# Delta rule in a two-layer fp32 kernel: decay products of levels 0 to 4 as packed 32 by 32 strips, put into the matrices by transfers; merges at 16 and 32 as 64 by 64 diagonal tiles

## The chip, the core and the metric

One core of a Trainium2 chip runs the whole program. It has TensorE (PE, with its weight loads shown apart as PEld), VectorE (DVE), ScalarE (ACT), GpSimd (POOL) and SyncE (SP), which issues every transfer here. The metric is the device time of one launch in microseconds (us): 1788.34 us as the median of three runs (1781.23, 1788.34, 1789.08).

## The reference, cut to what matters

The program is two layers on x of 1024 tokens by 256: windowed attention and a feed-forward block, then delta-rule attention and feed-forward, all in fp32. The change lies in the delta rule of layer 1, with 16 heads of width 128, whose recurrence is per token

```
S   = S * exp(g_t)[:, None]          # decay of each key channel
u_t = beta_t * (v_t - k_t^T S)       # the delta
S   = S + k_t u_t^T
o_t = q_t^T S
```

The kernel takes 128 tokens at a time (a chunk, 8 per head). In a chunk it needs two triangular matrices per head and chunk: M, of products of key i with key j and the decay between them, and the same with query i. Then it needs the inverse of (1 + M), since each delta depends on those before it.

## The kernel before, in words

**The decay products by levels.** A decay between two tokens is a product over the channels and can't be taken as one factor outside the matmul. So the matrix is built in 7 levels: at level lv the tokens are grouped into pairs of runs of s = 2^lv tokens, and only the block (left run, right run) of each pair is computed. After each level, `advance` multiplies the keys and queries by the decay of a run, so that the next level's product is right. Before, levels 0 to 5 were computed as 64 by 64 diagonal pieces of a 128-token chunk: `dr_level` on PE (L849) makes, for a group `gr` of four chunks, 8 matmuls with 64 columns of stationary keys each, two per chunk (they go to the upper and the lower 64 partitions of the bank). Each moves 64 columns (32 for keys and 32 for queries). PE runs an fp32 matmul as two passes, so the trace shows 16 instructions for it. DVE then picks, with a predicated copy under a mask (L1597), the blocks of the level out of 512 columns of the bank into MB, the matrix tile, for levels 0 to 4. Levels 5 and 6 are copied by ACT. `advance` is L1617 and L1619 on DVE. The two groups alternate, group 0 in bank 2 and group 1 in bank 3.

**The base inverse.** After level 3 the 16 by 16 diagonal blocks are complete. SP writes the 64 of them (8 chunks by 8 blocks) to DRAM in 8 transfers (L519) and reads them back (L523) as 64 rows, one block per partition. DVE inverts all 64 together in 29 short steps (`invert` L1697, `less` L1705 and L1708), ACT makes a transposed copy (`flip`, L1215). SP then writes both to DRAM (L531, L532) and puts them in 16 transfers (L538, L539) on the diagonals of XX (the inverse) and YY (its transpose).

**The merges.** From 16 the inverse grows to 32, 64 and 128: `left` (L869 at 16 and 32, L871 at 64) multiplies MB by XX, ACT negates the product into PM (L1201), `right` (L891 and L893, L887 at 64) multiplies that by YY and by XX's transpose, and DVE (L1636, L1639) copies the new blocks into XX and YY. At 16 and 32 these are matmuls over the full 128 by 128 array, 4 per `left` and 8 per `right` and group.

**The scan.** For each chunk in turn: `predict` (L912, L913), DVE subtracts (L1646), `solve` (L924), ACT copies (L1224), `update` (L931, L932), DVE adds (L1657).

**The order.** The order on each engine is written out by hand as the table `PLACE`: (time in heads, step), sorted over all heads, so steps of up to four heads stand beside each other. The engines wait for each other by semaphores, PE and DVE strictly in this order. SP has its own order, in `delta_rule_loads`: per head m, `zero` (waits for the last `left` of head m-1), `beta_of`, `head`, `blocks`, `inverse`, `gate_weights`. `inverse` waits for the last `less` and for `flip`. PE's `left` at 16 waits for the transfers of XX.

## Time and profile before

The profiled execution has a span of 1786.4 us, 1.9 us under the median of the three runs and between the lowest and the highest of them; what lies around its span isn't recorded apart.

| engine | busy us | share of the span |
|---|---|---|
| PE matmul | 1552.1 | 87% |
| PE weight load | 1073.6 | 60% |
| DVE | 1338.7 | 75% |
| ACT | 1034.0 | 58% |
| POOL | 41.3 | 2% |
| DMA queue of SP | - | 12.1% of 16 engines |

The delta rule takes from about 560 to 1710 us, and in its steady part a pair of heads takes 128.8 us. The program alternates between heads of even and of odd number, since the output projection is done every second head. A high busy share is an average: each stretch of a head has its own limit, so the rows below go by stretches. The clock that PE was granted is in the columns of the windows (1.00 is 2.4 GHz, 0.50 is 1.2 GHz).

### The profile page before, as it was taken

What the parts mean: (1) busy time and instruction counts of PE and PEld (TensorE: products, weight loads), DVE (VectorE), ACT (ScalarE), POOL (GpSimd) and SP (SyncE); (2) the same over time, 40 slices, a digit from 0 to 9 for tenths busy, and PEclk for the clock granted to TensorE, in tenths of its full rate; (3) what the DMA queues carried; (4) which work ended last, traced back from release to release, by engine and by line L of the source; (5) the groups of instructions that cost most, each with busy time, mean ns of one, the idle gap of its engine ahead of it and who ended that gap; (6) DMA issues with size and microseconds to landing.
All of it is one profiled execution on the core that took longest, in us unless ns stands there. A gap on an engine that the chain in (4) does not pass through costs nothing. (4 is left out here: it accounts for less than half of the span.)

```text
span 1786.4 us, 33061 instructions
## 1 busy us (share of the span) xinstructions
PE 1552.1 (87%) x10840; PEld 1073.6 (60%) x10840; DVE 1338.7 (75%) x3718; ACT 1034.0 (58%) x2716; POOL 41.3 (2%) x49
## 2 busy tenths in 40 slices
PE   6887888788797689999999999999899999988678
PEld 3434555564453256776776776677677677677435
DVE  5859989847722578989888898898998988983131
ACT  5428778766311556776586676676667657643210
POOL 0000000000000000000000000000000000000000
PEclk9989999899998789999999999999999999978589
DMA  3041000000101101101111110110110110100010
GB/s 152 25 100 49 8 10 4 2 1 1 74 0 40 66 12 41 55 11 57 59 23 45 58 56 11 57 56 12 61 54 16 57 54 15 45 28 7 0 50 24
DMA packets 83350, 66.79 MB, mean 37 GB/s; under 512 B 58592, under 2 KB 72160, under 8 KB 82032
## 3 DMA queue, kind: packets, MB, share of 16 engines
q1 hardware_dynamic: 83184, 64.69, 12.1%
q8 instruction: 91, 1.49, 0.4%
q14 instruction: 75, 0.61, 0.1%
HBM read 55.71 MB, written 6.98 MB: 35 GB/s over the span
## 5 line engine op out<-in xcount | busy, mean ns | idle before, releaser
L796 PE MATMUL bank<-xt,arena 128*128 128x512 f32 x384 | 204.7, 669 | 4.5 <-ACT arena L1106 3.1
L1539 DVE SCALAR_TENSOR_TENSOR arena<-arena 128x1024 f32<-128x1024 f32 x144 | 184.1, 1279 | 31.7 <-ACT arena L1114 30.9
L1597 DVE COPY_PREDICATED arena<-arena,bank 128x512 f32<-128x512 int32 x160 | 185.1, 1176 | 0.0
L849 PE MATMUL bank<-arena 128*64 128x64 f32 x3072 | 143.6, 238 | 36.8 <-DVE arena L1619 22.3
L849 PEld LDWEIGHTS bank<-arena 128*64 128x64 f32 x3072 | 116.9, 144 | 84.3 <-issue 55.4
L1617 DVE TENSOR_TENSOR arena<-arena 128x512 f32<-128x512 f32 x224 | 156.6, 699 | 3.8 <-PE bank L849 3.0
L646 PE MATMUL bank<-xt,arena 128*128 128x512 f32 x320 | 142.6, 602 | 3.8 <-DVE arena L1357 3.8
L796 PEld LDWEIGHTS bank<-xt,arena 128*128 128x128 f32 x384 | 76.2, 215 | 79.2 <-issue 76.4
L1113 ACT COPY arena<-bank 128x512 f32<-128x512 f32 x96 | 56.6, 589 | 99.0 <-PE bank L796 99.0
L646 PEld LDWEIGHTS bank<-xt,arena 128*128 128x128 f32 x320 | 60.4, 193 | 86.8 <-issue 86.6
L1047 ACT ACTIVATE arena<-arena 128x128 f32<-128x128 f32 x256 | 99.1, 389 | 6.6 <-DVE arena L1467 6.6
L665 PE MATMUL bank<-arena 128*128 128x256 f32 (+2 forms) x384 | 95.6, 395 | 6.2 <-DVE arena L1357 5.3
L893 PE MATMUL bank<-arena 128*128 128x64 f32 x512 | 99.5, 275 | 0.0
L891 PE MATMUL bank<-arena 128*128 128x64 f32 x512 | 96.5, 269 | 0.8 <-DVE arena L1639 0.5
L1224 ACT COPY arena<-bank 128x128 f32<-128x128 f32 x128 | 34.3, 268 | 104.6 <-PE bank L924 104.2
L1619 DVE TENSOR_TENSOR arena<-arena 128x256 f32<-128x256 f32 x224 | 94.3, 421 | 0.0
L1233 ACT COPY arena<-bank 128x128 f32<-128x128 f32 x128 | 34.1, 267 | 96.5 <-PE bank L932 59.2
L665 PEld LDWEIGHTS bank<-arena 128*128 128x128 f32 (+2 forms) x384 | 67.9, 189 | 34.8 <-issue 20.5
L693 PE MATMUL bank<-xt,arena 128*128 128x512 f32 x160 | 83.1, 648 | 5.3 <-DVE arena L1450 4.5
L891 PEld LDWEIGHTS bank<-arena 128*128 128x128 f32 x512 | 80.4, 194 | 9.7 <-DVE arena L1639 5.9
L912 PEld LDWEIGHTS bank<-arena 128*128 128x128 f32 x224 | 40.8, 199 | 67.1 <-issue 39.4
L893 PEld LDWEIGHTS bank<-arena 128*128 128x128 f32 x512 | 78.8, 194 | 0.0
(169 smaller groups left out, 3512.3 us busy)
## 6 DMA issues: line engine op xcount, KB each, us to landing
arena<-zero_scratch SPq DMA_DIRECT2D x29, 512.0 KB, 4.3
arena<-d_w SPq DMA_DIRECT2D x16, 519.0 KB, 6.2
arena<-beta_scratch SPq DMA_DIRECT2D x16, 512.0 KB, 5.5
arena<-w_scratch SPq DMA_DIRECT2D x2, 1376.0 KB, 6.1
arena<-f_idx SPq DMA_DIRECT2D x2, 1072.0 KB, 12.5
w_scratch<-arena SPq DMA_DIRECT2D x2, 1072.0 KB, 4.0
arena<-a_wq SPq DMA_DIRECT2D x16, 128.0 KB, 2.8
arena<-a_wo SPq DMA_DIRECT2D x1, 2048.0 KB, 10.8
```

Source lines behind the costliest of these rows:

```text
L646: last = pe.matmul(bank[2 * w + n % 2][0:rows, :], (WU if f < 2 else WU1R)[:, w, k, m * P:m * P + rows], XT[:, k, hf * HALF:(hf + 1) * HAL ...
L665: last = pe.matmul(bank[4 + pair][:, j * D:(j + 1) * D], HT[0:rows, hf, m, t * P:(t + 1) * P], (WD if f < 2 else WD1)[0:rows, m, :], start ...
L693: last = pe.matmul(bank[6 + m % 2][:], w, XT[:, k, hf * HALF:(hf + 1) * HALF], start=(k == 0), stop=(k == KC - 1))
L796: last = pe.matmul(bank[b][:], DW[:, par, c:c + P], XT[:, k, rhs], start=(k == 0), stop=(k == KC - 1))
L849: last = pe.matmul(to[:, :, p], KL[:, par, r], rhs, start=True, stop=True)
L891: pe.matmul(to[:, 0], YY[:, par, c, :], PM[:, c, :].rearrange("p (b r s) -> p b r s", r=2, s=s)[:, :, 0, :], start=True, stop=True)
L893: last = pe.matmul(to[:, 1], PM[:, c, :], YY[:, par, c, :].rearrange("p (b r s) -> p b r s", r=2, s=s)[:, :, 1, :], start=True, stop=True)
L1047: last = act.activation(EX[:, p % 2, i, a, :], SMK[:, p % 2, i, a, :], ACT.Exp, bias=NMX[:, p % 2, i, a:a + 1], scale=-1.0, accum_out=ES[: ...
L1539: dve.scalar_tensor_tensor(out=CT[:, x], in0=RAW[:, x, 3 - j:3 - j + S], scalar=DW[:, par, tap:tap + 1], in1=CT[:, x], op0=ALU.mult, op1=A ...
L1597: dve.copy_predicated(out, mask, bank[b][:].rearrange("p (c b s) -> p c b s", c=8, s=s)).then_inc(free[b], 1)
L1617: dve.tensor_tensor(kq, kq, left, ALU.mult)
L1619: dve.tensor_tensor(kl, kl, t[:, :, 1, :].broadcast_to([P, nb // 2, s]), ALU.mult).then_inc(kq_step, 1)
```

## The change

The matrices MB stay as they are, but levels 0 to 4 are computed into a packed tile MBC. A chunk of 128 tokens is four strips of 32 tokens, and strip k of the diagonal stands on partitions 32k to 32k+31, 32 columns wide. On PE a level is 16 matmuls per group instead of 8, each with 32 columns of stationary keys (to one quarter of the bank's partitions) and 32 moving columns. On DVE the predicated copy reads 128 columns instead of 512. After level 4, SP puts the strips into MB by four transfers of 32 partitions (`strips`), which stand between `blocks` and `inverse`. `left` at 16 waits for them too.

XX and PM keep only the two 64 by 64 diagonal blocks (64 columns). The merges at 16 and 32 are done per 64 by 64 block: `left` is 8 matmuls per group with 64 rows, 64 stationary and 64 moving columns instead of 4 over the full array, `right` is 16 with 64 rows, 64 stationary and 32 moving columns instead of 8. ACT's negation reads 256 columns instead of 512. DVE's copy into XX is 128 columns instead of 256, and the one into YY becomes two of 64 partitions by 128 columns. The masks are cut out of the input by eight small transfers instead of one. `PLACE` doesn't change.

```diff
@@ -42,6 +42,10 @@
 BASE = 4
 BLK = 1 << BASE
 NB = P // BLK
+STRIP = 2 * BLK
+HP = P // 2
+DR_CONST = 16 * (2 + P // STRIP + 4)
+STRIP_LEVELS = BASE + 1
 
...
         MB = A.take(2, NT, 2, P)
+        MBC = A.take(2, NT, 2, STRIP)
         YY = A.take(2, NT, P)
-        XX = A.take(NT, P)
-        PM = A.take(NT, P)
+        XX = A.take(NT, HP)
+        PM = A.take(NT, HP)
         VB = A.take(2, NT, P)
         KT = A.take(2, NT, P)
...
                     sp.dma_start(BL, blk_in.rearrange("b (j i) -> b j i", j=BLK)).then_inc(blocks_in, 16)
+
+                def strips(m, par):
+
+                    sp.wait_ge(strips_ready, 2 * m + 2)
+                    wait(sp, full[6], read(6, m - 2, "predict", NT - 1))
+                    for k in range(P // STRIP):
+                        ks = slice(STRIP * k, STRIP * (k + 1))
+                        sp.dma_start(MB[ks, par, :, :, ks], MBC[ks, par]).then_inc(strips_put, 16)
 
                 def inverse(m, par):
 
...
+                    strips(m, m % 2)
                     inverse(m, m % 2)
                     if m + 2 < H:
...
@@ -841,6 +864,13 @@
                     pe.wait_ge(kq_step, done("dve", n, "advance", lv - 1, gr))
                 for t in range(4):
                     c = 4 * gr + t
+                    if lv < STRIP_LEVELS:
+                        for k in range(P // STRIP):
+                            r = slice(c * P + STRIP * k, c * P + STRIP * (k + 1))
+                            rhs = KQ[:, par, :, r].rearrange("p w (b r s) -> p w b r s", r=2, s=s)[:, :, :, 1, :]
+                            to = bank[b][STRIP * k:STRIP * (k + 1), t * STRIP:(t + 1) * STRIP]
+                            last = pe.matmul(to.rearrange("p (w b s) -> p w b s", w=2, s=s), KL[:, par, r], rhs, start=True, stop=True)
+                        continue
                     if lv < LEVELS - 1:
                         for p in range(2):
                             r = slice(c * P + 64 * p, c * P + 64 * p + 64)
...
                     pe.wait_ge(x_put, 16 * NB * (n + 1))
-                    for high in range(BASE, LEVELS):
+                    pe.wait_ge(strips_put, 16 * (P // STRIP) * (n + 1))
+                    for high in range(STRIP_LEVELS, LEVELS):
                         pe.wait_ge(free[b], read(b, n, "level", high, gr))
                 else:
                     pe.wait_ge(x_sel, done("dve", n, "right", lv - 1, gr))
                 for t in range(4):
                     c = 4 * gr + t
                     if lv < LEVELS - 1:
-                        last = pe.matmul(bank[b][:, t * P:(t + 1) * P], MB[:, par, c, 0, :], XX[:, c, :], start=True, stop=True)
+                        for h in range(2):
+                            hs = slice(HP * h, HP * (h + 1))
+                            last = pe.matmul(bank[b][hs, t * HP:(t + 1) * HP], MB[hs, par, c, 0, hs], XX[hs, c, :],
+                                             start=True, stop=True)
                     else:
-                        last = pe.matmul(bank[b][64:P, t * 64:(t + 1) * 64], MB[0:64, par, c, 0, 64:P], XX[0:64, c, 0:64],
+                        last = pe.matmul(bank[b][HP:P, t * HP:(t + 1) * HP], MB[0:HP, par, c, 0, HP:P], XX[0:HP, c, :],
                                          start=True, stop=True)
                 last.then_inc(full[b], 1)
 
...
                     if lv == LEVELS - 1:
-                        last = pe.matmul(bank[4][0:64, t * 64:(t + 1) * 64], PM[64:P, c, 0:64], YY[64:P, par, c, 64:P],
+                        last = pe.matmul(bank[4][0:HP, t * HP:(t + 1) * HP], PM[HP:P, c, :], YY[HP:P, par, c, HP:P],
                                          start=True, stop=True)
                         continue
-                    to = bank[4][:, t * P:(t + 1) * P].rearrange("p (w b s) -> p w b s", w=2, s=s)
-                    pe.matmul(to[:, 0], YY[:, par, c, :], PM[:, c, :].rearrange("p (b r s) -> p b r s", r=2, s=s)[:, :, 0, :],
-                              start=True, stop=True)
-                    last = pe.matmul(to[:, 1], PM[:, c, :], YY[:, par, c, :].rearrange("p (b r s) -> p b r s", r=2, s=s)[:, :, 1, :],
-                                     start=True, stop=True)
+                    for w in range(2):
+                        for h in range(2):
+                            hs = slice(HP * h, HP * (h + 1))
+                            y = YY[hs, par, c, hs]
+                            to = bank[4][hs, t * HP + STRIP * w:t * HP + STRIP * (w + 1)].rearrange("p (b s) -> p b s", s=s)
+                            left, moved = (PM[hs, c, :], y) if w else (y, PM[hs, c, :])
+                            moved = moved.rearrange("p (b r s) -> p b r s", r=2, s=s)[:, :, w, :]
+                            last = pe.matmul(to, left, moved, start=True, stop=True)
                 last.then_inc(full[4], 1)
 
             def dr_keys(n, par, gr):
...
                 if lv < LEVELS - 1:
-                    act.mul(PM[:, cg, :], bank[b][:].rearrange("p (c k) -> p c k", c=4), -1.0).then_inc(free[b], 1)
+                    act.mul(PM[:, cg, :], bank[b][:, 0:4 * HP].rearrange("p (c k) -> p c k", c=4), -1.0).then_inc(free[b], 1)
                 else:
...
@@ -1582,22 +1619,22 @@
             def dr_level(n, par, lv, gr):
 
                 b = 2 + gr
-                dve.wait_ge(dr_const, 48)
+                dve.wait_ge(dr_const, DR_CONST)
                 dve.wait_ge(full[b], turn(b, n, "level", lv, gr) + 1)
                 if lv == 0:
-                    wait(dve, full[6], read(6, n - 2, "predict", NT - 1))
+                    wait(dve, strips_put, 16 * (P // STRIP) * (n - 1))
                 else:
                     dve.wait_ge(free[b], read(b, n, "level", lv - 1, gr))
                 if lv == BASE:
                     dve.wait_ge(blocks_out, 16 * NB * (n + 1))
                 s = 1 << lv
-                out = MB[:, par, 4 * gr:4 * gr + 4].rearrange("p c w (b r s) -> p (c w) b r s", r=2, s=s)[:, :, :, 1, :]
-                mask = MKU[:, lv, :].rearrange("p (a b s) -> p a b s", a=1, s=s).broadcast_to([P, 8, 64 // s, s])
+                out = MBC[:, par, 4 * gr:4 * gr + 4].rearrange("p c w (b r s) -> p (c w) b r s", r=2, s=s)[:, :, :, 1, :]
+                mask = MKC[:, lv, :].rearrange("p (a b s) -> p a b s", a=1, s=s).broadcast_to([P, 8, BLK // s, s])
                 dve.memset(TICK[:, 6 + 2 * lv + gr:7 + 2 * lv + gr], 0.0)
-                dve.copy_predicated(out, mask, bank[b][:].rearrange("p (c b s) -> p c b s", c=8, s=s)).then_inc(free[b], 1)
-                if lv == BASE - 1:
+                dve.copy_predicated(out, mask, bank[b][:, 0:4 * STRIP].rearrange("p (c b s) -> p c b s", c=8, s=s)).then_inc(free[b], 1)
...
+                if lv >= BASE - 1:
                     dve.wait_ge(free[b], read(b, n, "level", lv, gr))
-                    dve.memset(TICK[:, 18 + gr:19 + gr], 0.0).then_inc(blocks_ready, 1)
+                    dve.memset(TICK[:, 16 + 2 * (lv - BASE + 1) + gr:17 + 2 * (lv - BASE + 1) + gr], 0.0).then_inc((blocks_ready, strips_ready)[lv - BASE + 1], 1)
 
             def dr_advance(n, par, lv, gr):
...
@@ -1632,11 +1669,14 @@
                     dve.wait_ge(y_put, 16 * NB * (n + 1))
                 dve.memset(TICK[:, 18 + 2 * lv + gr:19 + 2 * lv + gr], 0.0)
                 x = XX[:, cg, :].rearrange("p c (b r s) -> p c b r s", r=2, s=s)[:, :, :, 0, :]
-                mask = MKL[:, lv, :].rearrange("p (a b s) -> p a b s", a=1, s=s).broadcast_to([P, 4, 64 // s, s])
+                mask = MKX[:, lv - BASE, :].rearrange("p (a b s) -> p a b s", a=1, s=s).broadcast_to([P, 4, STRIP // s, s])
                 dve.copy_predicated(x, mask, prod[:, :, 0]).then_inc(x_sel, 1)
-                y = YY[:, par, cg, :].rearrange("p c (b r s) -> p c b r s", r=2, s=s)[:, :, :, 1, :]
-                mask = MKU[:, lv, :].rearrange("p (a b s) -> p a b s", a=1, s=s).broadcast_to([P, 4, 64 // s, s])
-                dve.copy_predicated(y, mask, prod[:, :, 1]).then_inc(free[4], 1)
+                for h in range(2):
+                    hs = slice(HP * h, HP * (h + 1))
+                    y = YY[hs, par, cg, hs].rearrange("p c (b r s) -> p c b r s", r=2, s=s)[:, :, :, 1, :]
+                    mask = MKY[hs, lv - BASE, :].rearrange("p (a b s) -> p a b s", a=1, s=s).broadcast_to([HP, 4, STRIP // s, s])
+                    last = dve.copy_predicated(y, mask, prod[hs, :, 1])
+                last.then_inc(free[4], 1)
 
             def dr_predict(n, par, c):
```

SyncE around the transfers of one head (before; the third head of the delta rule). `blocks` is L519 and L523, `inverse` L531 to L539:

```order
68 L519 DMA block_scratch<-arena 16x8x16 [waits blocks_in,blocks_ready]
69 L519 DMA block_scratch<-arena 16x8x16 x7
70 L523 DMA arena<-block_scratch 64x256 [waits base_step,blocks_out]
71 L531 DMA inverse_scratch<-arena 64x256 [waits x_put,y_put,flipped,base_step]
72 L532 DMA inverse_turned_scratch<-arena 64x256
73 L538 DMA arena<-inverse_turned_scratch 16x8x16 [waits x_zero,inverse_out]
```

The same place now, with the strips as L545:

```order
71 L533 DMA block_scratch<-arena 16x8x16 [waits blocks_in,blocks_ready]
72 L533 DMA block_scratch<-arena 16x8x16 x7
73 L537 DMA arena<-block_scratch 64x256 [waits base_step,blocks_out]
74 L545 DMA arena<-arena 32x16x32 [waits strips_ready]
75 L545 DMA arena<-arena 32x16x32 x3
76 L553 DMA inverse_scratch<-arena 64x256 [waits x_put,y_put,flipped,base_step]
77 L554 DMA inverse_turned_scratch<-arena 64x256
78 L560 DMA arena<-inverse_turned_scratch 16x8x16 [waits x_zero,inverse_out]
```

The four transfers and their wait for level 4 now stand ahead of the inverse's way out to DRAM, and each has 32 by 16 pieces of 32 elements.

TensorE at the first merge of a head, before (bank2 and bank3 are `left` of the two groups, bank4 is `right`, bank5 and bank6 are the scan of another head):

```order
1104 L869 MATMUL bank2<-arena 128x128 x4
1105 L869 MATMUL bank3<-arena 128x128 x4
1106 L931 MATMUL bank5<-arena 128x128
1107 L932 MATMUL bank6<-arena 128x128
1108 L891 MATMUL bank4<-arena 128x64
1109 L893 MATMUL bank4<-arena 128x64
1110 L891 MATMUL bank4<-arena 128x64
1111 L893 MATMUL bank4<-arena 128x64
```

And now:

```order
964 L902 MATMUL bank2<-arena 64x64 x8
965 L902 MATMUL bank3<-arena 64x64 x8
966 L968 MATMUL bank5<-arena 128x128
967 L969 MATMUL bank6<-arena 128x128
968 L931 MATMUL bank4<-arena 64x32 x16
969 L835 MATMUL bank1<-arena 128x512
```

The steps stand in the same order; each `left` has twice the matmuls with half the columns, and so has each `right`, in runs of 16 (L931 now, L891 and L893 before).

## Rows read from the trace of the kernel before

**Rows 1.** Windows (us; then per engine busy us and count; then PEclk, DMA share, GB/s).

```profile
979.30:998.30 19.00, 19.00 (x148) 17.20 (x146) 14.67 (x30) 12.91 (x25) 0.00 (x0) 1.00 0.06 17
998.30:1015.70 17.40, 15.73 (x200) 12.05 (x199) 16.96 (x40) 10.34 (x26) 1.63 (x1) 1.00 0.34 123
1015.70:1044.40 28.70, 25.85 (x167) 16.42 (x166) 25.50 (x67) 19.96 (x47) 0.00 (x0) 0.94 0.11 15
1044.40:1059.90 15.50, 15.50 (x129) 14.15 (x128) 13.26 (x28) 12.58 (x25) 0.00 (x0) 1.00 0.02 5
1059.90:1077.40 17.50, 15.82 (x201) 12.10 (x199) 17.05 (x40) 10.34 (x26) 1.64 (x1) 1.00 0.34 122
1077.40:1108.10 30.70, 28.89 (x183) 19.41 (x182) 26.80 (x69) 20.43 (x47) 0.00 (x0) 0.94 0.10 15
```

**Rows 2.** Timeline of DVE: start us, us, line, operation, shapes, count.

```profile
983.57 0.51 DVE L1636 COPY_PREDICATED arena<-arena,bank 128x256 f32<-128x256 int32 x1
...
999.11 1.33 DVE L1597 COPY_PREDICATED arena<-arena,bank 128x512 f32<-128x512 int32 x1
1000.23 0.73 DVE L1617 TENSOR_TENSOR arena<-arena 128x512 f32<-128x512 f32 x1
...
1020.66 0.86 DVE L1597 COPY_PREDICATED arena<-arena,bank 128x512 f32<-128x512 int32 x1
```

**Rows 3.** Timeline of PE at 202 us (attention, tiles of 64 by 64).

```profile
201.48 0.67 PE L713 MATMUL bank<-arena 64*64 64x128 f32 x16
202.08 0.44 PE L726 MATMUL bank<-ident,arena 128*128 128x128 f32 x2
```

**Rows 4.** Timeline of PE, merges and levels.

```profile
986.65 1.06 PE L869 MATMUL bank<-arena 128*128 128x128 f32 x8
987.55 1.89 PE L958 MATMUL bank<-arena 128*128 128x256 f32 x8
...
992.34 0.33 PE L891 MATMUL bank<-arena 128*128 128x64 f32 x2
...
994.17 0.38 PE L938 MATMUL bank<-arena 128*1 128x128 f32 x2
...
1002.12 0.73 PE L849 MATMUL bank<-arena 128*64 128x64 f32 x16
1002.78 0.67 PE L887 MATMUL bank<-arena 64*64 64x64 f32 x8
1003.38 0.49 PE L924 MATMUL bank<-arena 128*128 128x128 f32 x2
...
1013.27 0.69 PE L849 MATMUL bank<-arena 128*64 128x64 f32 x16 [0.26 <-DVE arena L1619]
```

**Rows 5.** Timelines of SP, then DVE, then PE, around the inverse of one head.

```profile
1015.73 3.63 SPq L519 DMA_DIRECT2D block_scratch<-arena  x8
...
1033.07 0.45 SPq L531 DMA_DIRECT2D inverse_scratch<-arena  x1
...
1042.80 0.42 SPq L539 DMA_DIRECT2D arena<-inverse_scratch  x1
...
1031.46 0.18 DVE L1708 TENSOR_TENSOR arena<-arena 64x14 f32<-64x14 f32 x1
...
1034.11 0.86 DVE L1597 COPY_PREDICATED arena<-arena,bank 128x512 f32<-128x512 int32 x1
...
1044.38 1.80 PE L869 MATMUL bank<-arena 128*128 128x128 f32 x14
```

**Rows 6.** Line L587 on SP: transfers of 512 pieces (duration ns min/median/max, starts).

```profile
L587 SPq DMA_DIRECT2D arena<-arena x4: 652/1068/1200, 120.7 to 126.5; - x4
```

**Rows 7.** PE after its longest wait in the delta rule, and the clock there.

```profile
660.60 3.75 PE L869 MATMUL bank<-arena 128*128 128x128 f32 x16 [3.78 <-issue]
...
663.00:667.00 4.00, 4.00 (x21) 4.00 (x20) 0.00 (x0) 2.74 (x4) 0.00 (x0) 0.50 0.02 4
```

36 lines of the change are left out of this document (23 added, 13 removed).

## The prediction

> **What bounds the kernel now.** I read the windows of two neighbouring heads first, cut at three events: the first `left` at 16, the first level, and the way out of the 16 by 16 blocks [rows 1]. The pair takes 128.8 us. The reader is to see three stretches with three different limits. From `left` to level 0 (19.0 and 15.5 us) PE is busy without a gap. From level 0 to the blocks (17.4 and 17.5 us) DVE is busy for 16.96 of 17.40 and PE for 15.73. From the blocks to the next `left` (28.7 and 30.7 us) neither is full; there a chain runs: blocks out and in, 29 short DVE steps, inverse out, 16 transfers in, `left`. The timelines of SP, DVE and PE show that chain [rows 5]: blocks leave at 1015.73, the last `less` starts at 1031.46, the inverse leaves at 1033.07, the last transfer is issued at 1042.80, and `left` starts at 1044.38, which leaves 1.6 us for that transfer to land. So in this head PE arrives at `left` when the data does. The next head's stretch is 2 us longer, since it holds two more projections; PE comes last there.
>
> **The levels on DVE.** The predicated copy of 512 columns at level 0 keeps DVE from 999.11 to 1000.23, 1.12 us; at level 4, where runs are long, one lasts 0.86 us, and a copy of 256 columns of that kind 0.51 us [rows 2]. On that line 128 columns last 0.33 us; I take 0.3. Ten copies per head save 8 x 0.82 + 2 x 0.5 = 7.6 us of DVE, of which 6.6 lie in the stretch that DVE bounds. DVE is left with 10.4 us there, so PE is next.
>
> **The levels on PE.** A group of 16 passes costs 0.66 us, start to start (1002.12 to 1002.78) [rows 4]. It becomes 32 passes of half the columns, on four tiles. No row shows this form. The ends: if four tiles run at once and each pass costs by its columns, 32 passes take half of the 0.51 us that 16 take without the last one's own length, so 0.45 us with start and end. If a pass can't start more often than in the attention's group, 16 passes of 128 columns on four tiles in 0.67 us less 0.27 for the last [rows 3], 27 ns each, then 32 take 0.85 + 0.19 = 1.04 us. Below 0.45 it can't fall while the columns set it. I take the middle, 0.75 us, +0.09 per group. From level 0's start (998.3) to the last of the eight groups (1013.27) it is 15.0 us [rows 4], of which PE waits most of 1.7 [rows 1]. With DVE fast 1.2 of the wait goes: 15.0 - 1.2 + 7 x 0.09 = 14.4, and 1.1 us for that group and its copy (2.4 before, as DVE was behind). The stretch becomes 15.5 instead of 17.4.
>
> **The merges on PE.** `left` at 16 or 32 costs 0.90 us (986.65 to 987.55), `right` 1.83 us (992.34 to 994.17) [rows 4]. Now they run on two 64 by 64 tiles in turn. The nearest row is again the level group of two tiles with 64 columns: 0.66 us for 16 passes, so 0.66 for `left`, and 0.66 + 0.49 = 1.15 for the 32 passes of `right`, whose stationary part has 64 columns too. Four of each per head save 4 x 0.24 + 4 x 0.68 = 3.7 us. The other end, one tile after the other, is the rival below. In the stretch of 19.0 us this gives 15.3, and DVE's 14.67 lies close below, so 15.6; in the one of 15.5 PE would need 11.8, but DVE has 13.26, so 13.4. There DVE's extra copy into YY (two of 64 partitions instead of one, 0.3 each) and the smaller copy into XX cancel. ACT's negation gets shorter beside PE's work: nothing.
>
> **The new wait.** SP's queue goes: blocks, strips, inverse. The strips need level 4 of group 1, whose copy starts at 1034.11 [rows 5], 2.65 us after the last `less`; the inverse left at 1033.07. With a copy of 0.3 and its tick the strips can go at 1034.6, 1.5 us after the inverse left before. Then come four transfers of 512 pieces. The attention has such transfers (512 pieces, of 512 bytes): 0.65 us to issue the first, 1.07 in the middle, 1.20 at most [rows 6]. The last transfer of an inverse, with 128 pieces, took 0.42. The ends are 4 x 0.45 = 1.8 and 4 x 1.1 = 4.4; the pieces here are of 128 bytes and start on an idle queue, so I take 4 x 0.65 + gaps = 2.7. Behind the waiting instruction stand the inverse's two transfers, its 16, the weights of the gate and the zeroing for the next head; only the first two kinds are waited for, by `left`. Landing behind the strips' bytes I give 0.3 (0 to 2). DVE reaches the inversion earlier by the shorter copy at level 4 and what it waits less: 0.8 (0.5 to 1). Sum: 1.5 + 2.7 + 0.3 - 0.8 = +3.7, so 28.7 becomes 32.4 us, now in both heads. PE would come to `left` at 30.2 and 32.2 (28.7 and 30.7, plus 1.3 as the blocks leave sooner after PE's last group, plus 0.2 for two groups), so it is late by the chain by 2.2 and 0.2 us. What was PE's slack is gone.
>
> **The sum.** A pair: 15.6 + 13.4 + 2 x 15.5 + 2 x 32.4 = 124.8 us. To this 1 us for the clock: after a wait of 3.78 us PE ran at 0.50 for the whole of the next window, and two `left` took 3.75 us [rows 7] instead of twice 0.90. A wait of 2.2 us is shorter, so I charge little. 125.8 against 128.8 is 1.5 us per head, times 15 about 22 us. At the start eight small transfers for masks instead of one and a memset more cost about 1 us. The first and the last head have empty engines around; there the shorter levels and the longer chain cancel. The profiled execution has 1786.4 us of span, 1.9 below the median; I subtract from the latter: 1788 - 22 = **1766 us**.
>
> **Rival 1, the full gain.** The four tiles run at once (0.45 us per group) and the transfers cost 1.8 us. Then the second stretch is 13.4, the chain 31.4, and PE comes last at 32.2 in every second head: 29.0 + 26.8 + 63.6 = 119.4, 4.7 us per head, **1717 us**. For it: groups with two and with four tiles both go as their columns say. Against: nothing so far shows passes as short.
>
> **Rival 2, slower: the two diagonal tiles don't overlap.** The two tiles of a merge have different rows of the array and write the same bank. In the attention, tiles of different rows write different banks; the level groups have two tiles with the same rows. A group on one single tile (L887) takes 0.60 us for 8 passes, 1002.78 to 1003.38 [rows 4], 65 ns per pass. `left` then costs 1.12, `right` 2.16, and each stretch after `left` grows by 4 x 0.22 + 4 x 0.33 = 2.2 instead of shrinking: 21.2 + 17.7 + 31.0 + 64.8 = 134.7, 3 us per head, **1832 us**. It decides as soon as a merge pass goes above 50 ns, since then the 1.5 us of gain are spent. The Trainium skill has the rule behind it, "TensorEngine Tiling (Array Packing)", section "Restrictions and Gotchas": different row tiles can't access the same PSUM bank at the same time. By that rule the time is this rival's, without it the forecast's; no row here tests it, as the attention's code avoids the case.
>
> **Rival 3, slower: the wait takes over.** The transfers take 1.07 us each to issue and 2 us more to land: the chain is 35.9 us, PE waits over 3 us in each head, and the clock falls as in [rows 7]. 7 us more per pair and 2 for the clock: 133.8, 2.5 us per head, **1825 us**. For it: SP has nothing between the blocks and the inverse now, so each microsecond counts in full. Against: the pieces are a quarter of the attention's.
>
> **Rival 4, no gain: the passes don't get shorter.** At 1.04 us per level group the second stretch is 17.5 as before and PE comes to `left` later, which hides the chain: 129.4, **1793 us**. The even pace of 27 ns in [rows 3] speaks for it as much as for columns. The Trainium skill says the same from its side: "TensorE: Matmul & The Clock Gate", section "Wait — 56ns, not 53.3ns?", has a floor of about 25 ns from start to start however few the columns. By that floor 32 passes would be an estimated 0.99 us and the time this rival's; the trace shows 34 and 27 ns per pass, never less, so it doesn't refute it.
>
> **Chances.** Forecast 0.40 (its own range 1745 to 1785), rival 1 0.15, rival 2 0.15, rival 3 0.12, rival 4 0.18 (1775 to 1810). A difference under 0.5%, 9 us, is no change here. Faster: 0.32 + 0.15 + 0.05 = 0.52. Same: 0.08 + 0.02 + 0.07 = 0.17. Slower: 0.15 + 0.10 + 0.06 = 0.31. The range reaches from under rival 1 to rival 2, 1712 to 1832.
>
> **What would show it.** The predicated copy of the levels near 0.3 us; a level group's 32 passes in 0.45, 0.75 or 1.04 us; `left` in 0.66 and `right` in 1.15 us, or near 1.1 and 2.2; the first strip transfer 1.5 us after the inverse used to leave, 0.65 us each; PE idle right before `left` at 16, by 2 us in one head of two, and whether its clock falls after that. The stretch from blocks to `left` should be near 32 us in both heads. If it stays at 29 to 31, the wait was hidden; if DVE still fills the second stretch, its copies didn't shrink with the columns, and the forecast fails there.

## The result, and the profile after

The changed kernel takes 1813.8 us as the median (1797.3 to 1819.9), the kernel before 1788.7 (1781.2 to 1789.5): a ratio of 1.0134 with a 95% interval of 1.0083 to 1.0184. It is slower by 1.3%. The forecast was 1766 us, faster by 1.2%. The profiled execution has a span of 1813.3 us (1786.4 before).

The totals moved as they were meant to, and the time didn't follow. TensorE's matmuls are busy for 32 us less (1519.7), VectorE for 99 us less (1239.9). The page of the changed kernel, its line of the engines and one group (for the group: busy us and mean ns, then the idle time ahead of it and what ended that):

```profile
PE 1519.7 (84%) x14936; PEld 1014.4 (56%) x14936; DVE 1239.9 (68%) x3815; ACT 1025.5 (57%) x2716; POOL 41.2 (2%) x49
...
L902 PE MATMUL bank<-arena 64*64 64x64 f32 x1024 | 50.4, 258 | 58.0 <-issue 55.2
```

L902 is `left` at 16 and 32. TensorE stands idle for 58.0 us ahead of it, in the trace of before 4.9 us. That is a new wait of (58.0 - 4.9) / 15 = 3.5 us per head. The six windows of the same two heads show where it lies and what comes with it, against [rows 1] (columns as there: PE, PEld, DVE, ACT, POOL busy, then PEclk, DMA share, GB/s):

```profile
990.05:1006.87 16.82, 15.52 (x240) 12.37 (x241) 12.85 (x29) 12.82 (x26) 0.00 (x0) 1.00 0.08 22
1006.87:1020.32 13.45, 12.66 (x319) 9.46 (x319) 11.56 (x41) 9.29 (x25) 1.63 (x1) 1.00 0.40 141
1020.32:1053.39 33.07, 24.66 (x206) 16.08 (x205) 26.50 (x71) 20.42 (x48) 0.00 (x0) 0.97 0.14 21
1053.39:1069.87 16.48, 15.32 (x225) 12.12 (x225) 11.65 (x27) 11.45 (x24) 0.00 (x0) 0.76 0.02 5
1069.87:1087.24 17.37, 17.02 (x319) 12.70 (x319) 11.65 (x41) 10.68 (x26) 1.63 (x1) 0.71 0.32 109
1087.24:1122.16 34.92, 29.18 (x221) 19.84 (x221) 27.80 (x73) 20.80 (x48) 0.00 (x0) 0.95 0.13 20
```

The first two rows are what the change can do: 16.82 and 13.45 us, where before took 19.00 and 17.40, both at full clock. The third and sixth are the queue: 33.07 and 34.92 us for 28.70 and 30.70. The fourth and fifth are the same steps as the first two (the fourth has less to do, as in [rows 1]), at a granted clock of 0.76 and 0.71. They took 16.48 and 17.37, where before took 15.50 and 17.50, at 1.00.

Call the three stretches A (`left` at 16 to level 0), B (level 0 to the blocks) and C (blocks to `left`). To compare kernels I use their means over 13 heads (heads 2 to 14, counted from 0) of one trace each, with the time at the lower clock (PEclk 0.50, which is 1.2 GHz, against 1.00, which is 2.4 GHz) in brackets: 2 x (1 - PEclk) x the length of the window. The median is of all runs. The ratio to before is an estimate of its own, with an interval, and not the quotient of the two medians; it differs from that by up to 0.5%. One of the five runs of the strips from ACT (1765.1 us) counts as slow; without it their median is 1748 us.

| kernel | A | B | C | sum | median us | ratio |
|---|---|---|---|---|---|---|
| before | 17.1 (0) | 17.5 (0) | 29.7 (3.4) | 64.4 | 1789 | 1 |
| changed | 17.9 (7.1) | 15.1 (4.7) | 33.5 (2.2) | 66.5 | 1814 | 1.0134 |
| strips, old merges | 19.1 (4.0) | 13.3 (0) | 33.5 (2.0) | 65.8 | 1808 | 1.0093 |
| merges alone | 15.1 (0) | 19.8 (6.0) | 30.3 (3.6) | 65.1 | 1799 | 1.0055 |
| strips from ACT | 15.0 (0) | 16.0 (6.8) | 32.3 (2.9) | 63.3 | 1752 | 0.9741 |
| strips behind the inverse | 16.3 (3.4) | 16.0 (7.1) | 31.2 (1.1) | 63.4 | 1755 | 0.9769 |
| strips from POOL | 15.0 (0) | 15.8 (6.8) | 30.0 (0.5) | 60.8 | 1725 | 0.9617 |
| same, old merges | 17.1 (0) | 13.3 (0) | 29.5 (0.5) | 59.9 | 1718 | 0.9605 |
| strips from POOL, wait filled | 28.6 for both (0) | | 29.9 (0.8) | 58.5 | 1693 | 0.9471 |

### The profile page after: what moved, and what is told of

Same layout as the page of the kernel before. It is cut to its first block and busy times, and to the rows that moved or that the text cites. A ratio compares the mean times of both kernels' runs of the same rounds, so it can differ in the third digit from the quotient of the medians.

```text
span 1813.3 us, 41435 instructions
## 1 busy us (share of the span) xinstructions
PE 1519.7 (84%) x14936; PEld 1014.4 (56%) x14936; DVE 1239.9 (68%) x3815; ACT 1025.5 (57%) x2716; POOL 41.2 (2%) x49
## 5 line engine op out<-in xcount | busy, mean ns | idle before, releaser
L1576 DVE SCALAR_TENSOR_TENSOR arena<-arena 128x1024 f32<-128x1024 f32 x144 | 184.6, 1282 | 32.4 <-ACT arena L1151 31.0
L819 PE MATMUL bank<-xt,arena 128*128 128x512 f32 x384 | 195.3, 642 | 5.4 <-ACT arena L1143 4.0
L669 PE MATMUL bank<-xt,arena 128*128 128x512 f32 x320 | 143.3, 604 | 3.8 <-DVE arena L1394 3.8
L688 PE MATMUL bank<-arena 128*128 128x256 f32 (+2 forms) x384 | 100.2, 409 | 6.2 <-DVE arena L1394 5.3
L902 PE MATMUL bank<-arena 64*64 64x64 f32 x1024 | 50.4, 258 | 58.0 <-issue 55.2
L872 PEld LDWEIGHTS bank<-arena 128*32 128x32 f32 x5120 | 62.4, 120 | 65.4 <-issue 51.8
L1697 DVE SCALAR_TENSOR_TENSOR arena<-arena,bank 128x128 f32<-128x128 f32 x112 | 38.7, 345 | 87.0 <-PE bank L968 84.9
L872 PE MATMUL bank<-arena 128*32 128x32 f32 x5120 | 77.5, 209 | 23.2 <-DVE arena L1617 14.0
L949 PEld LDWEIGHTS bank<-arena 128*128 128x128 f32 x224 | 43.1, 213 | 89.8 <-issue 56.0
L931 PEld LDWEIGHTS bank<-arena 64*64 64x64 f32 x2048 | 79.3, 159 | 24.2 <-DVE arena L1678 14.6
L716 PE MATMUL bank<-xt,arena 128*128 128x512 f32 x160 | 87.5, 677 | 6.3 <-DVE arena L1487 5.6
L931 PE MATMUL bank<-arena 64*64 64x32 f32 x2048 | 86.1, 241 | 2.1 <-DVE arena L1678 2.0
L949 PE MATMUL bank<-arena 128*128 128x128 f32 x224 | 53.2, 323 | 38.1 <-DVE arena L1697 31.2
```

Source lines behind the costliest of these rows:

```text
L669: last = pe.matmul(bank[2 * w + n % 2][0:rows, :], (WU if f < 2 else WU1R)[:, w, k, m * P:m * P + rows], XT[:, k, hf * HALF:(hf + 1) * HAL ...
L688: last = pe.matmul(bank[4 + pair][:, j * D:(j + 1) * D], HT[0:rows, hf, m, t * P:(t + 1) * P], (WD if f < 2 else WD1)[0:rows, m, :], start ...
L716: last = pe.matmul(bank[6 + m % 2][:], w, XT[:, k, hf * HALF:(hf + 1) * HALF], start=(k == 0), stop=(k == KC - 1))
L819: last = pe.matmul(bank[b][:], DW[:, par, c:c + P], XT[:, k, rhs], start=(k == 0), stop=(k == KC - 1))
L872: last = pe.matmul(to.rearrange("p (w b s) -> p w b s", w=2, s=s), KL[:, par, r], rhs, start=True, stop=True)
L931: last = pe.matmul(to, left, moved, start=True, stop=True)
```

## The experiments

**Where the queue's time goes.** The timeline of SP of the changed kernel around the inverse of that head, against [rows 5]:

```profile
1020.32 3.63 SPq L533 DMA_DIRECT2D block_scratch<-arena  x8
...
1038.70 2.67 SPq L545 DMA_DIRECT2D arena<-arena  x4
1041.54 0.52 SPq L553 DMA_DIRECT2D inverse_scratch<-arena  x1
...
1044.17 0.31 SPq L560 DMA_DIRECT2D arena<-inverse_turned_scratch  x1
...
1052.13 0.43 SPq L561 DMA_DIRECT2D arena<-inverse_scratch  x1
```

The inverse leaves 21.2 us after the blocks (1041.54 - 1020.32) instead of 17.3 (1033.07 - 1015.73). TensorE then arrives early and waits, and what happens to its clock is in the timeline of PE and in four windows around it: the work before the wait, the wait, the work behind it, and work later in the same stretch.

```profile
1053.39 1.97 PE L902 MATMUL bank<-arena 64*64 64x64 f32 x32 [4.79 <-issue]
...
1063.97 0.68 PE L902 MATMUL bank<-arena 64*64 64x64 f32 x16
1064.49 1.07 PE L931 MATMUL bank<-arena 64*64 64x32 f32 x32
...
1069.87 0.49 PE L872 MATMUL bank<-arena 128*32 128x32 f32 x32 [1.16 <-DVE arena L1617]
```

```profile
1043.50:1048.60 5.10, 4.52 (x22) 2.94 (x22) 4.80 (x8) 4.00 (x9) 0.00 (x0) 1.00 0.15 20
1048.60:1053.39 4.79, 0.00 (x1) 0.04 (x1) 1.50 (x3) 0.27 (x1) 0.00 (x0) 0.77 0.19 18
1053.39:1061.14 7.75, 7.75 (x74) 6.09 (x74) 3.75 (x10) 3.75 (x8) 0.00 (x0) 0.50 0.04 9
1062.30:1068.50 6.20, 6.20 (x122) 4.82 (x118) 5.44 (x15) 5.29 (x13) 0.00 (x0) 1.00 0.00 0
```

The clock is 1.00 up to the wait, falls in it, and is 0.50 for 7.75 us of full work behind it. The price of the wait is therefore the 4.79 us of standing still and then up to half of those 7.75. The first six experiments take this apart.

**1. The wait alone, in the kernel before.** SP waits for level 4 and issues four transfers of unused data, and nothing gets shorter.

```diff
+                def strips(m, par):
+                    sp.wait_ge(strips_ready, 2 * m + 2)
+                    wait(sp, strips_put, 64 * m)
+                    for k in range(4):
+                        ks = slice(32 * k, 32 * (k + 1))
+                        sp.dma_start(JUNK[ks, :, :, ks], MBC[ks, par]).then_inc(strips_put, 16)
...
+                    strips(m, m % 2)
                     inverse(m, m % 2)
```

> The kernel before with nothing changed but SyncE's queue: between blocks and inverse it waits for level 4 of both groups and then issues four transfers of 512 pieces of 128 bytes each to a tile that nobody reads. Theory 1: blocks to left from 29.7 to about 34 us, TensorE stalls of 3 to 6 us before left, half clock after them, left to level 0 longer than 17.1 though nothing in it changed, by 1 to 4 us; time 1788 + 16 x 5 to 8 = 1870 to 1915 us. Theory 2 (the clock or a stall does no harm of its own): left to level 0 stays at 17.1, time at most 1788 + 16 x 4.5 = 1860.

Measured: 1886.5 us, ratio 1.0550 (1.0522 to 1.0577), +98 us. C grew from 29.7 to 34.1, and A from 17.1 to 19.3, with 4.4 us at the lower clock, though nothing in A was changed. The windows of one head (A, B, C):

```profile
1157.17:1177.81 20.64, 20.64 (x144) 18.84 (x144) 12.93 (x27) 12.65 (x24) 0.00 (x0) 0.92 0.07 17
1177.81:1195.29 17.48, 15.81 (x200) 12.12 (x198) 17.00 (x40) 10.35 (x26) 1.63 (x1) 0.99 0.34 122
1195.29:1230.01 34.72, 27.38 (x167) 17.76 (x167) 27.50 (x71) 20.23 (x48) 0.00 (x0) 0.89 0.13 20
```

So the wait costs 4.3 us in its own stretch (34.05 against 29.75) and 2.1 in the next one (19.26 against 17.12). The time lies in the range of theory 1.

**2. Work in the wait.** TensorE runs 10 (even heads) or 6 unneeded matmuls of 256 columns before it waits for the inverse; its waits for the banks of levels 5 and 6 are moved ahead of the filling. The queue is as in the changed kernel.

```diff
+                    if gr == 0:
+                        for _ in range(FILL[n % 2]):
+                            pe.matmul(bank[b][:, 256:512], ident[:], XT[:, 0, 0:256], start=True, stop=True)
                     pe.wait_ge(x_put, 16 * NB * (n + 1))
```

> The changed kernel with matmuls that nobody needs (10 in even heads, 6 in odd ones, 128 by 128 by 256, about 4.3 and 2.6 us at full clock) into an unused half of the bank just before TensorE waits for the inverse at left 16. They fill the stall and change nothing that follows. Theory 1: the clock stays at 1.0 after left, left to level 0 from 17.9 to 14.5 to 15.5 us, blocks to left unchanged near 33.5; time 1814 - 16 x 2.5 to 3.5 = 1758 to 1775 us. Theory 2 (merges' own form makes the stretch long): left to level 0 stays at 17.9, time 1805 to 1830 us.

Measured: 1786.8 us, ratio 0.9994 (0.9966 to 1.0021): 27 us less than the changed kernel, for 128 matmuls more. The chain wasn't touched (C is 33.6), so this is the part of the loss that is clock alone. From the blocks over the filling to level 0 there is almost no time at the lower clock left (0.5 + 0.5 us per head, 2.2 + 7.1 in the changed kernel). A is 15.2, as theory 1 had it; but the time is above its range (1758 to 1775), and B still has 5.2 us at the lower clock.

**3. No strips in the queue at all.** This kernel leaves out the transfers that bring levels 0 to 4 into the matrices, and the waits for them; only its time is read.

```diff
-                    strips(m, m % 2)
...
-                    pe.wait_ge(strips_put, 16 * (P // STRIP) * (n + 1))
```

> The changed kernel without the four strip transfers and the waits for them (levels 0 to 4 never reach the matrices, so that part of the computation is left out). It bounds what all of the transfers cost. Theory 1: as with the transfers on ScalarE's queue or a few us less, 1705 to 1735 us. Theory 2: near 1750 us.

Measured: 1718.2 us, ratio 0.9610 (0.9578 to 0.9641). C is 29.5, A 15.1, B 15.7. Together with experiment 1 this puts the loss against the kernel before on four transfers and their wait. It isn't all that is lost: B has 6.5 us at the lower clock here too, without any strips.

**4. The strips from ScalarE's queue.**

```diff
-        (1.809, "flip"), (1.903, "level", 5, 1), (1.92, "gate", 0), (1.963, "level", 6, 0), (1.972, "level", 6, 1),
+        (1.809, "flip"), (1.85, "strips"), (1.903, "level", 5, 1), (1.92, "gate", 0), (1.963, "level", 6, 0), (1.972, "level", 6, 1),
...
-                    strips(m, m % 2)
...
+                    act.dma_start(MB[ks, par, :, :, ks], MBC[ks, par]).then_inc(strips_put, 16)
```

> The changed kernel with the four strip transfers issued from ScalarE's queue (after flip), so that SyncE's queue is as before: blocks, inverse. Theory 1 (the wait and the transfers in SyncE's queue delay the inverse, TensorE stalls 2 to 5 us before left at 16, and its clock falls afterwards): blocks to left back from 33.5 to 28.5 to 31 us, hardly any stall, left to level 0 down from 17.9 to about 14.5 us, time near 1715 us (1700 to 1740). Theory 2 (the form of the merges, 64 by 64 tiles between full ones, is what made left to level 0 longer): only blocks to left shrinks, by 4 us per head at most, left to level 0 stays near 17.9, time near 1750. Theory 3 (bytes of the strips, whichever queue): no change from 1814.

Measured: 1751.9 us, ratio 0.9741 (0.9704 to 0.9778). That is outside the 1700 to 1740 of theory 1 and near the 1750 of theory 2, but A is 15.0, which theory 2 had at 17.9. The wait ahead of `left` is gone, yet C is 32.3, not 29.5. ACT's timeline shows why: the issue occupies the engine, and the scan's copies stand behind it.

```profile
1143.35 0.65 ACTq L1251 DMA_DIRECT2D arena<-arena  x1
...
1144.03 2.03 ACTq L1251 DMA_DIRECT2D arena<-arena  x3
1146.11 1.06 ACT L1158 ACTIVATE arena<-arena 128x1024 f32<-128x1024 f32 x1 [1.61 <-issue]
1147.07 0.25 ACT L1269 COPY arena<-bank 128x128 f32<-128x128 f32 x1
1147.22 0.28 ACT L1270 ACTIVATE arena<-bank 128x128 f32<-128x128 f32 x1
```

And PE's, which waits for that last one:

```profile
1147.64 0.49 PE L940 MATMUL bank<-arena 128*128 128x128 f32 x2 [1.96 <-ACT arena L1270]
```

The cost was moved to another queue, not removed.

**5. The strips from GpSimd's queue.** GpSimd has one small operation per head in the delta rule.

```diff
-    "pool": [
+    "pool": [(1.85, "strips"), 
         (3.32, "stats"),
...
+                    pool.dma_start(MB[ks, par, :, :, ks], MBC[ks, par]).then_inc(strips_put, 16)
```

> The changed kernel with the four strip transfers issued from GpSimd's queue, which has nothing else in the delta rule but one small operation per head. With them on ScalarE the time was 1752 us, with none at all 1718 us. Theory 1 (what was left there, 2.8 us per head in the third stretch, is ScalarE standing still for the 2.7 us of the issues while the scan waits for it): the third stretch falls from 32.3 to 29.5 to 30.5 us and the time is 1720 to 1735 us. Theory 2 (what is left is the strips' own way, from level 4 until they have landed): the third stretch stays at 32 us and the time at 1750 us, with a wait of TensorE right before left at 16 or before level 5.

Measured: 1725.3 us, ratio 0.9617 (0.9586 to 0.9648). C is 30.0. POOL's timeline has the issues at the same length, with nobody behind them:

```profile
1131.76 2.62 POOL L1323 DMA_DIRECT2D arena<-arena  x4 [33.78 <-DVE tick L1636]
```

The second theory (that the strips' own way holds `left` up) falls: it would have left C at 32. What this costs over no strips at all is 7 us in the whole program.

**6. The strips one place further back in SP's queue**, behind the two transfers that take the inverse out.

```diff
                     sp.dma_start(blk_x.rearrange("b (i c) -> b i c", i=BLK), ZT).then_inc(inverse_out, 16)
+                    strips(m, par)
                     sp.wait_ge(inverse_out, 32 * (m + 1))
```

> The changed kernel with the strips still in SyncE's queue, but issued after the two transfers that take the inverse out and before the wait for them. The way out and its landing take about 2.9 us in the kernel before (1033.07 to the first put at 1036), so most of the strips' 2.7 us of issue lie beside it. Theory 1 (the loss is the strips' time ahead of the inverse in this queue): the inverse leaves at +16.5 us after the blocks, as before, the puts start at +21.3 instead of +24.9, the stall ahead of left falls from 3.7 to about 1 us, and the time is 1750 to 1765 us. Theory 2 (any wait of TensorE here brings the clock down, its length matters little): 1785 us or more.

Measured: 1755.4 us, ratio 0.9769 (0.9729 to 0.9810), inside the range of theory 1. The inverse leaves at +17.0 us after the blocks (mean of 13 heads), as before, and the first of the puts into YY starts at +22.5, against +20.0 before and +25.4 in the changed kernel. One line moved wins 58 us. But it isn't as good as POOL: a wait of up to 2.8 us stays ahead of `left` in most of the heads, and A has 3.4 us of lower clock.

**7. The strips without the merges.** The changed kernel with the full-array merges of before: XX and PM have their 128 columns again, and `left`, `right`, ACT's negation and DVE's copies are those of before.

```diff
-        XX = A.take(NT, HP)
-        PM = A.take(NT, HP)
+        XX = A.take(NT, P)
+        PM = A.take(NT, P)
...
-                        for h in range(2):
-                            hs = slice(HP * h, HP * (h + 1))
-                            last = pe.matmul(bank[b][hs, t * HP:(t + 1) * HP], MB[hs, par, c, 0, hs], XX[hs, c, :],
-                                             start=True, stop=True)
+                        last = pe.matmul(bank[b][:, t * P:(t + 1) * P], MB[:, par, c, 0, :], XX[:, c, :], start=True, stop=True)
```

> The changed kernel with the full-array merges of before: only the levels as strips, with the transfers in SyncE's queue. Theory 1: the second stretch stays at 15.1 us, the third at 33.5 us or a little more, and the first is 17.1 plus the 2.8 us by which the changed kernel's was above what its merges need, 19.9: 68.5 us per head against 64.4, so about 1850 us (1835 to 1865). Theory 2 (the merges are the loss): below 1813 us, near 1775.

Measured: 1808.4 us, ratio 1.0093 (1.0067 to 1.0119), where I expected 1850. Its windows for the head of the first table (A, B, C):

```profile
988.70:1009.34 20.64, 20.64 (x144) 18.84 (x144) 12.96 (x27) 12.63 (x24) 0.00 (x0) 0.92 0.07 17
1009.34:1022.52 13.18, 12.65 (x321) 9.48 (x319) 11.06 (x40) 10.34 (x26) 1.64 (x1) 1.00 0.48 162
1022.52:1055.78 33.26, 24.65 (x205) 16.08 (x205) 26.42 (x71) 20.39 (x48) 0.00 (x0) 0.99 0.14 21
```

B is the surprise. I expected 15.1, as in the changed kernel; it is 13.3 at full clock in every head (mean of 13). So the strips are worth 4.2 us per head in B, not the 2.4 that the changed kernel shows. And with the same strips and the same queue, the merges made the kernel no faster: 1808 without, 1814 with them. That fits neither theory: the first had 1850, and the second, which allows anything below 1813, had 1775.

**8. The merges without the strips**, in the kernel before: the lines of experiment 7 the other way round.

> The kernel before with only the merges at 16 and 32 changed: two diagonal tiles of 64 by 64; the levels and SyncE's queue stay as they were, so there is no new wait. Theory 1 (the merges' saving is real, the loss of the changed kernel is the strips' wait and the clock behind it): left 0.61 and right 1.17 us as in the changed kernel, the stretch from left to the first level 15.0 us instead of 17.1, the other two 17.5 and 29.7 as before, so 2.1 us per head and about 1755 us (1745 to 1765), and no stall ahead of left at 16 over 1 us. Theory 2 (the rise of that stretch to 17.9 us in the changed kernel comes from the merges themselves, twice as many matmuls in runs of 16): the stretch is 17.5 us or more here too and the time 1788 us or above.

Measured: 1798.9 us, ratio 1.0055 (1.0031 to 1.0079): slower, where I expected 1755. The first half of the expectation holds: A is 15.1. But B, in which nothing was changed, went from 17.5 to 19.8. The timeline of PE at the border of A and B, and windows of the 3.6 us before the wait, the wait, and the stretch behind it:

```profile
1061.33 0.45 PE L884 MATMUL bank<-arena 64*64 64x64 f32 x5
1062.93 1.12 PE L859 MATMUL bank<-arena 128*64 128x64 f32 x16 [1.16 <-DVE arena L1596]
```

```profile
1058.17:1061.77 3.60, 3.23 (x52) 2.04 (x48) 3.49 (x10) 3.57 (x7) 0.00 (x0) 1.00 0.02 5
1061.77:1062.93 1.16, 0.01 (x1) 0.03 (x1) 1.12 (x3) 1.13 (x4) 0.00 (x0) 0.92 0.00 0
1062.93:1077.39 14.46, 14.46 (x111) 11.32 (x111) 11.05 (x25) 7.39 (x20) 1.63 (x1) 0.53 0.36 129
```

L859 is level 0: a group of 16 passes takes 1.12 us here, 0.73 in [rows 4]. TensorE, now quicker with its merges, is done before VectorE's last product of the keys (L1596) and waits 1.16 us for it, and behind that wait it runs at the lower clock for most of 14.5 us. In the kernel before there is no such wait. The fall doesn't come in every head: with a wait of 1.10 to 1.16 us in each of the 13, five heads have less than 0.6 us at the lower clock in B and the others 6.8 to 13.5. Two readings were left: the short wait brings the clock down, or the long run of small diagonal tiles before it does. The next three runs tell them apart.

**9. The wait without the tiles.** The kernel before with two more products on VectorE.

```diff
+                    dve.tensor_tensor(JUNK[:, 0:8].rearrange("p c k -> p (c k)"), BB, BB, ALU.mult)
+                    dve.tensor_tensor(JUNK[:, 8:12].rearrange("p c k -> p (c k)"), BB[:, 0:4 * P], BB[:, 0:4 * P], ALU.mult)
                     dve.tensor_tensor(KL[:, par], KL[:, par], BB, ALU.mult).then_inc(key_step, 1)
```

> The kernel before with two more products on VectorE (1024 and 512 columns, 1.85 us, into unused memory) ahead of the last product of the keys, on which level 0 waits. Nothing else is changed: full-array merges, 16 passes per level group. It opens the wait that TensorE has ahead of level 0 in every kernel with the diagonal merges (1.16 us) and hasn't in the kernel before. In those kernels the second stretch ran 5 to 7 us at the lower clock (1.2 GHz), in the two with full-array merges 0. Theory 1 (the short wait brings the clock down): TensorE waits 1.2 to 1.8 us ahead of level 0, the first stretch grows by 1.3 us, and the second has 5 to 7 us of low clock and grows by 2.3: about 1840 us. Theory 2 (the diagonal tiles before the wait do): the second stretch stays at 17.5 us with no low clock; about 1808 us.

Measured: 1835.6 us, ratio 1.0260 (1.0215 to 1.0304). A is 18.2 with no lower clock, B 19.4 with 6.3 us of it. The same border, with full-array merges ahead of the wait (L892, L894):

```profile
1216.04 0.39 PE L894 MATMUL bank<-arena 128*128 128x64 f32 x2
1216.35 0.68 PE L872 MATMUL bank<-arena 64*64 64x64 f32 x8
1218.08 1.12 PE L850 MATMUL bank<-arena 128*64 128x64 f32 x16 [1.05 <-issue]
```

```profile
1208.00:1217.03 9.03, 9.03 (x77) 8.05 (x75) 8.53 (x16) 7.48 (x16) 0.00 (x0) 1.00 0.01 2
1217.03:1218.08 1.05, 0.01 (x1) 0.04 (x1) 1.05 (x3) 0.99 (x2) 0.00 (x0) 0.96 0.00 0
1218.08:1224.60 6.52, 6.52 (x64) 5.72 (x66) 5.30 (x13) 2.83 (x8) 1.63 (x1) 0.50 0.11 16
```

After 9 us without a gap, one wait of 1.05 us is enough. In 12 of the 13 heads 3.4 to 10.2 us at the lower clock follow it in B, in one head none. The expected 1.3 us of the longer stretch came as 1.1, and the other 1.9 us are the clock: 47 us on the kernel for 1.85 us of VectorE per head.

**10 and 11. The wait filled**, in the kernel with the strips from POOL: with 5 full-array matmuls of 128 columns, or with 18 on the two diagonal tiles in turn.

```diff
                 use(b, n, "level", lv, gr)
                 if lv == 0:
+                    if gr == 1:
+                        for _ in range(5):
+                            pe.matmul(bank[b][:, 256:384], ident[:], XT[:, 0, 0:P], start=True, stop=True)
                     pe.wait_ge(key_step, done("dve", n, "key", 2))
```

> The changed kernel with the strips issued by GpSimd (1725 us, first and second stretch 15.0 and 15.8 us, the latter with 6.8 us at the lower clock), and five more matmuls of 128 by 128 per head (full array, 1.1 us, into a part of the bank that nobody reads) in TensorE's wait of 1.16 us ahead of level 0. Theory 1 (that wait brings the clock down): the low clock in the second stretch goes, it takes 13.3 us as with full-array merges, 1685 to 1695 us. Theory 2 (the long run of diagonal tiles does): the low clock stays, 1720 to 1730 us.

> As the one before, but the wait is filled with 18 matmuls on the two 64 by 64 diagonal tiles in turn (1.1 us). Theory 1 (any wait brings it down, any work holds it): as with full-array filling, 1685 to 1695 us. Theory 2 (work on diagonal tiles counts for less): the low clock stays while full-array filling removes or shortens it, 1720 to 1730 us.

Measured: 1693.0 us (ratio 0.9471, 0.9422 to 0.9521) and 1700.0 us (0.9496, 0.9454 to 0.9537). A and B together take 28.6 us in both, with no time at the lower clock; without the filling 30.8. The second is 5 us above the range that I gave, but the intervals of the two overlap, so nothing shows that work on small tiles counts for less. PE's timeline of the first, where the wait of 1.16 us stood, and its windows A, B and C of one head:

```profile
1136.95 0.45 PE L899 MATMUL bank<-arena 64*64 64x64 f32 x5
1137.34 1.38 PE L854 MATMUL bank<-xt,ident 128*128 128x128 f32 x10
1138.65 0.49 PE L866 MATMUL bank<-arena 128*32 128x32 f32 x32
```

```profile
1125.04:1137.34 12.30, 11.72 (x226) 9.31 (x225) 11.91 (x28) 10.92 (x23) 0.00 (x0) 1.00 0.04 8
1137.34:1152.02 14.68, 13.97 (x331) 10.64 (x329) 12.76 (x43) 11.18 (x29) 1.67 (x1) 1.00 0.37 128
1152.02:1183.22 31.20, 27.60 (x221) 19.02 (x220) 26.03 (x71) 20.63 (x47) 2.62 (x4) 1.00 0.18 24
```

This is the best kernel of the study: both parts of the change, POOL's queue for the strips, and 5 unneeded matmuls per head. It beats the kernel before by 96 us and the changed one by 121.

**12. The strips from POOL with the old merges**, the lines of experiments 5 and 7 together.

> The levels as strips, issued by GpSimd, and the full-array merges of before: the levels' part of the change without the queue and without the diagonal merges. Theory 1 (the merges save 2.1 us per head in the first stretch and give back 2.5 in the second through the clock): first 17.1, second 13.3 with no low clock, third 30.0: 60.4 us per head against 60.8 with the diagonal merges, so 1715 to 1725 us. Theory 2 (the merges are worth their 2.1 us): 1755 to 1760 us.

Measured: 1718.4 us, ratio 0.9605 (0.9563 to 0.9648), as theory 1 had it. A is 17.1, B 13.3, both at full clock. So the strips are worth 70 us once nothing waits for their transfers, and the diagonal merges on top of them are worth nothing that can be told (1725 us) until the wait that they open is filled (1693).

## Why the prediction was wrong

**The levels on DVE: right, and larger.** The predicated copy takes 0.42 us on average (L1634, 160 times, 63.8 us in all; 185.1 before), 0.12 above the 0.3 that I took, and 0.33 at level 4. B is no longer bound by VectorE (11.1 of 13.2 us).

**The levels on PE: right in kind, too dear.** I took 0.75 us for a group of 32 passes. From its start to the next start it takes 0.39 us as the median of 49 groups at full clock, and 0.48 at most. The median lies below my lower end of 0.45, under which I had said that it can't fall. Four tiles of 32 output partitions each run side by side, 8 to 10 ns from one pass to the next within a group. The timeline of the changed kernel has one such group and what follows it:

```profile
1021.99 0.46 PE L872 MATMUL bank<-arena 128*32 128x32 f32 x32
1022.38 1.99 PE L819 MATMUL bank<-xt,arena 128*128 128x512 f32 x4
```

Rival 4 is refuted. The Trainium skill ("TensorE: Matmul & The Clock Gate", section "Wait — 56ns, not 53.3ns?") has a floor of about 25 ns from start to start, by which I weighed that rival. For passes on different tiles this trace shows no such floor. B at full clock is 13.3 us, not 15.5.

**The merges on PE: right.** At full clock `left` takes 0.61 us (0.66 forecast) and `right` 1.00 to 1.05 (1.15), 28 to 31 ns per pass. Rival 2 is refuted: the two diagonal tiles overlap although they write one bank. The rule of the Trainium skill that different row tiles can't access one bank at the same time ("TensorEngine Tiling (Array Packing)", section "Restrictions and Gotchas") doesn't bind here; these tiles differ in their rows and in the partitions that they write, and no run tested tiles that differ in rows alone.

**The new wait: right in kind, too small.** This is the first step that failed. I put the chain at +3.7 us: 1.5 for level 4, 2.7 + 0.3 for the transfers, less 0.8 for an earlier VectorE. The means of 13 heads say: the strips start 19.1 us after the blocks, the inverse used to leave at 17.0, so 2.1 us; the strips and gaps take 3.0 (22.1 - 19.1), a transfer 0.64 as forecast; the last put ends at 32.6 instead of 27.5. The sum is +5.1. The credit of 0.8 never came: the last `less` ends at +16.1 as before (+16.0), since the stretch before it is a chain over DMA and SP, which no faster copy shortens. So C became 33.5, not 32.4, and the wait of TensorE ahead of `left` 1.8 to 5.1 us (heads 4 to 12), not 2.2 and 0.2.

**The clock: the term that turned the sign.** I charged 1 us per pair on the grounds that 2.2 us is shorter than the 3.78 us of [rows 7]. What the runs show is that waits as short as 1.05 us (experiment 9) and 1.16 us (experiment 8) were followed by 0.50. In the changed kernel TensorE runs 14.0 us per head at the lower clock, against 3.4 before. A alone was forecast at 14.5 us and needs 15.0 at full clock; it took 17.9. B was forecast at 15.5, needs 13.3 and took 15.1. The two together lose 4.7 us per head against what they take at full clock. That is an estimate of the clock's price in these stretches, as A and B at full clock were read from different kernels.

**The sum again, by its own steps.** Per head: A +3.4 against the forecast, B -0.4, C +1.1: 66.5 instead of 62.4 (62.9 with the clock's charge). The forecast's gain of 64.4 - 62.9 = 1.5 us per head became a loss of 2.1, times 16 about 34 us; measured 25. By cause, the 3.6 us between 62.9 and 66.5 are C with 1.1, A at full clock with 0.5, the clock in A and B with 4.7 less the 0.5 charged, and B at full clock with -2.2. So the clock is the term that failed most, and the levels' better price hid part of it. Nearest stood rival 3 (1825 us, the wait takes over and the clock falls), to which I gave 0.12. It had the right mechanism, but 2 us per pair for the clock where some 9 were paid, and the wrong reason for the wait's size (issues of 1.07 us each; they took 0.64).

**What no part of the prediction had.** An engine that is made faster just ahead of a wait for another engine turns its gain into idle time. I set PE's 15.3 us in A beside DVE's 14.67, took 15.6, and called the difference to 19.0 a gain. I didn't ask what the wait between them does to the clock of the stretch behind it. Experiment 8 shows it without any strips: -2.1 us in A, +2.3 in B.

**What stays open.** Why one wait of 1.1 us brings the clock down and the same wait in another head doesn't is shown by no run here. Nor is the start: in the profiled execution of the changed kernel level 0 of the first head starts at 625.6 us, before at 615.8, though hardly anything ahead of it was changed, and in the other variants with strips between 617.7 and 624.6. That doesn't explain the loss, though. At `left` of head 1 the lag is down to 4.2 us, from there to `left` of head 15 the changed kernel loses 27.9, and behind that it gains 5.2 back: 26.9 us between the two spans. The kernel before has 3.4 us per head at the lower clock in C, and the one with the strips from POOL 0.5. In the trace of before it begins within 2.3 us of the blocks in 11 of the 13 heads, behind a B in which TensorE stands idle for 1.7 us of 17.4 [rows 1]; what causes it wasn't tested.

## What to carry to other kernels

Before a transfer is put into a queue, write down what stands behind it and how long the issues last: four issues of 0.64 us and a wait of 2.1 cost 96 us in SP's queue, 30 to 34 in ScalarE's and 7 in GpSimd's, which was idle. Before TensorE is made faster, look at whom it waits for next, and count a wait that it gets as its length plus the slower work behind it; where PEclk falls after a wait, a few unneeded matmuls in the wait are worth a run. And when two edits come together, run each alone, and then without the wait that it opens. Here each edit alone made the kernel slower (by 0.9% and 0.6%); the strips turned out to be worth 4% once their transfers left SP's queue, and the merges about 1.4% more once the wait behind them was filled.

## What the runs showed of the hardware that I had not expected

- A wait of 1.05 us after 9 us of gapless work was followed by a granted clock of 0.50 for all of the next 6.5 us (experiment 9). Filling a wait of 1.16 us with matmuls whose result nobody reads kept the clock at 1.00 and made the kernel 32 us faster (experiment 10 against 5).
- The fall doesn't follow each such wait: the window of head 6 in the changed kernel, 1006.87 to 1020.32 us, is at 1.00 throughout behind a wait of 1.11 us, and so is B in one head of 13 in experiment 9.
- Passes on four tiles of 32 output partitions start 8 to 10 ns apart at full clock, so 32 of them take 0.39 to 0.48 us to the next start.
- A transfer's issue takes nearly the same time on three queues: 2.67 us for four on SP, 2.71 on ACT and 2.62 on POOL in the heads shown, with a median for one of 0.64, 0.65 and 0.65 us, for 512 pieces of 128 bytes. The longest four of a head took 3.8, 4.1 and 6.5 us.
